# Two cross attentions: scores of two chunks together with their low part on halves of the array, and other places for the second loop's token and key work

## The reference, cut to what matters

```python
# inside the second block (a2): 32 wide heads, x [8,56,128], ee = ctx_512 [8,1500,64]
xn = _ln(x, lnx_g, lnx_b)
yn = _ln(y, lny_g, lny_b)
q = jnp.einsum('bsc,hcd->bhsd', xn, wq)
k = jnp.einsum('btc,hcd->bhtd', yn, wk)
v = jnp.einsum('btc,hcd->bhtd', yn, wv)
a = jax.nn.softmax(jnp.einsum('bhsd,bhtd->bhst', q, k) * D ** (-0.5), axis=-1)
o = jnp.einsum('bhst,bhtd->bhsd', a, v)
...
# the fifth block: 8 wide heads
qh = (q @ Wq + bq).reshape(B, LQ, HEADS, D_K).transpose(0, 2, 1, 3)
kh = (k @ Wk + bk).reshape(B, LKV, HEADS, D_K).transpose(0, 2, 1, 3)
vh = (v @ Wv + bv).reshape(B, LKV, HEADS, D_K).transpose(0, 2, 1, 3)
attn = jax.nn.softmax(jnp.einsum('bhqd,bhkd->bhqk', qh, kh) * scale, axis=-1)
out = jnp.einsum('bhqk,bhkd->bhqd', attn, vh)
```

## Time and profile before

| what | value |
|---|---|
| device time, median of 3 runs | 628.56 us (625.13 to 633.34) |
| the profiled execution, its time | 629.66 us |
| its span from first to last instruction | 627.8 us |
| first loop, a batch in the middle | 24.52 us |
| second loop, a batch in the middle | 22.69 us |
| PE, DVE, ACT, POOL busy over the span | 566.9, 444.7, 372.0, 380.6 us |

### The profile page before, as it was taken

One profiled execution on the slowest core, in us unless ns is written; L12 is line 12 of the kernel. 1 busy time (PEld: TensorE's weight loads), 2 busy tenths in 40 slices (PEclk: granted clock), 3 DMA queues, 4 the chain that ended last, 5 costly groups with the idle time before them and its releaser, 6 DMA issues.

```text
span 627.8 us, 18969 instructions
## 1 busy us (share of the span) xinstructions
PE 566.9 (90%) x8256; PEld 416.1 (66%) x8256; DVE 444.7 (71%) x698; ACT 372.0 (59%) x623; POOL 380.6 (61%) x271
## 2 busy tenths in 40 slices
PE   9788898899999999999888979977889889889897
PEld 4566775566767767666777556664667767778765
DVE  3876728697887887786356774776888988986543
ACT  2335674657657667566462417474677777777552
POOL 1572451488989889864630231175999999977500
PEclk9789999999999999999999999997999999999998
DMA  5830015002101101010013000412422432330000
GB/s 169 238 133 2 3 40 180 2 1 42 34 7 41 26 15 40 3 40 3 2 60 123 2 0 3 99 39 64 103 67 45 96 78 52 78 77 4 2 1 15
DMA packets 33838, 31.81 MB, mean 51 GB/s; under 512 B 27124, under 2 KB 27380, under 8 KB 33756
## 3 DMA queue, kind: packets, MB, share of 16 engines
q1 hardware_dynamic: 33756, 30.60, 18.8%
HBM read 13.06 MB, written 0.23 MB: 21 GB/s over the span
## 4 chain that ended last, share of the span: by engine, by line
PE 62%; DVE 18%; ACT 8%; issue 7%; POOL 3%; DMA 1%; DVEq 0%; POOLq 0%; ACTq 0%
PE psum L1143 9%; DVE scratch L1306 6%; PE psum L1067 5%; PE psum L1119 5%; PE psum L1503 4%; PE psum L1112 4%; PE psum L1114 4%; PE psum L1526 4%; DVE scratch L1291 4%; PE psum L217 3%; POOL scratch L1291 2%; ACT scratch L1276 2%; POOL scratch L652 1%; PE psum L1073 1%; PE psum L248 1%
## 5 line engine op out<-in xcount | busy, mean ns | idle before, releaser
L1291 POOL TENSOR_TENSOR scratch<-scratch 125x896 bf16<-125x896 f32 x143 | 242.7, 1715 | 80.4 <-ACT scratch L1276 79.9
L1306 DVE TENSOR_REDUCE scratch<-psum 128x1 f32<-128x500 f32 x336 | 210.3, 672 | 23.1 <-PE psum L1067 9.6
L1276 ACT ACTIVATE scratch<-psum 125x896 f32<-125x896 f32 x192 | 173.6, 917 | 82.8 <-PE psum L1143 51.1
L1112 PE MATMUL psum<-tok_high,scratch 125*128 125x65 bf16 x1344 | 107.0, 194 | 3.3 <-issue 2.7
L1114 PE MATMUL psum<-tok,scratch 125*128 125x64 bf16 x1344 | 106.4, 194 | 0.0
L1112 PEld LDWEIGHTS psum<-tok_high,scratch 125*128 125x128 bf16 x1344 | 94.8, 98 | 13.9 <-ACT scratch L1276 6.0
L1114 PEld LDWEIGHTS psum<-tok,scratch 125*128 125x128 bf16 x1344 | 88.6, 98 | 17.1 <-issue 0.5
L1143 PE MATMUL psum<-scratch 65*128 65x448 bf16 (+1 forms) x384 | 87.3, 352 | 0.0
L1291 DVE TENSOR_TENSOR scratch<-scratch 125x896 bf16<-125x896 f32 x49 | 67.5, 1383 | 22.8 <-ACT scratch L1276 21.1
L1119 PE MATMUL psum<-tok_high,scratch 125*128 125x65 bf16 x1344 | 72.7, 194 | 4.8 <-POOL scratch L1291 3.1
L1503 PE MATMUL psum<-scratch 128*128 128x500 bf16 x168 | 64.2, 382 | 10.8 <-DVE scratch L1306 6.5
(11 more groups left out here) (340 smaller groups left out, 870.5 us busy)
## 6 DMA issues: line engine op xcount, KB each, us to landing
nrm<-scratch SPq DMA_DIRECT2D x64, 96.0 KB, 2.2
nrm<-w_third SPq DMA_DIRECT2D x32, 96.0 KB, 2.2
raw<-ctx_dram SPq DMA_DIRECT2D x4, 672.0 KB
w_third<-fifth_dram SPq DMA_DIRECT2D x3, 595.0 KB, 6.0
w_third<-third_dram SPq DMA_DIRECT2D x2, 844.0 KB, 8.9
w_third<-third_dram SPq DMA_DIRECT2D x2, 843.5 KB, 6.8
w_fourth<-fourth_dram SPq DMA_DIRECT2D x3, 542.5 KB, 5.8
scratch<-scratch SPq DMA_DIRECT2D x8, 192.0 KB, 2.6
```

The costliest lines, as they stand in the source:

```text
L1112: nc.tensor.matmul(psum[:, sums, 65 * r:65 * r + 65], rows, t1[:, c, :], start=(c == 0 and r == 0), stop=False, skip_group_check=True)
L1276: nc.scalar.activation(CR["p"][0:CP, n % RING, :].rearrange("p (f n) -> p f n", f=2), psum[0:CP, S:S + 2, 0:HALF], ACT.Exp).then_inc(self. ...
L1291: ops.tensor_tensor(CR["pl"][0:CP, n % RING, :], CR["p"][0:CP, n % RING, :], p_high(n % RING), ALU.subtract).then_inc(done, 1)
L1306: nc.vector.tensor_reduce(mxp[:, r, t:t + 1], bank(B, TB), X_AXIS, ALU.max).then_inc(self.aux_freed, 1)
```

## The change

First loop. `scores_pe` does two chunks at each even step and nothing at the odd one: four matmuls over 128 rows, then four over 64 rows. The tiles `yb` and `qb` now hold the operands twice over: rows 0 to 63 for the first 448 columns, rows 64 to 127 for the second, so that these matmuls use one half of the array each. The row of ones and the shift move from row 64 to rows 0 and 64. For this channel 0 of the tokens has to go from the low product: `fold_keys_pool` subtracts the key weights' column 0 from all, once, on POOL. SP copies `yb` by two DMAs, 63 rows each. The shift is made and copied in halves of 448. Before it, ACT waits for DVE's low part of the queries.

Both loops. The rounding of the tokens to bfloat16 goes from POOL to ACT (`high_tokens`). POOL keeps the scaling (chunk 1) and the low parts: in the first loop both in chunk 11, in the second both in chunk 5. ACT does its part in chunks 4 and 5 of the first loop, 2 and 4 of the second.

Second loop. DVE does the roundings of chunks 5 and 6 instead of 1 and 2 (1 and 2 still in batch 0). The maxima are spread otherwise, the three key units of batch 0 stand in chunks 0 and 1, and SP turns the tokens of batch 2 before the groupings of batch 1.

```diff
+        def fold_keys_pool(pool):
+
+
+            keys = par("a2_wk").rearrange("p (h d) -> p h d", d=65)
+            nc.gpsimd.tensor_copy(keys[:, :, 64:65], keys[:, :, 0:1]).then_inc(key_scaled, 1)
+            pool.wait_ge(key_scaled, 2)
+            nc.gpsimd.tensor_tensor(keys[:, :, 0:64], keys[:, :, 0:64], keys[:, :, 64:65].to_broadcast([128, HEADS, CD]),
+                                    ALU.subtract).then_inc(key_scaled, 1)
+            pool.wait_ge(key_scaled, 3)
+
...
+                for k in range(2):
+                    nc.gpsimd.memset(CR["yb", i][64 * k:64 * k + 1, :].bitcast(F32), ONES).then_inc(y_ones, 1)
+                    pool.wait_ge(y_ones, 2 * i + k + 1)
...
+                    for r in range(3 * k, 3 * k + 4):
+                        lo, hi = max(128 * r, HALF * k), min(128 * r + 128, HALF * k + HALF)
+                        mm = nc.tensor.matmul(psum[:, B, lo - HALF * k:hi - HALF * k],
+                                              nmx[:, r:r + 1].to_broadcast([128, 128]),
+                                              ident16[:, lo - 128 * r:hi - 128 * r], start=True, stop=True)
...
+                if n % 2:
+                    return
+                b, i = n // CHUNKS, n // CHUNKS % 2
...
+                for m in (n, n + 1):
+                    if m >= 2:
+                        pe.wait_ge(self.probs, m - 1)
                     for f in range(2):
-                        mm = nc.tensor.matmul(bank(S + f, HALF), lhs[0:rows, 128 * c:128 * c + 128],
-                                              rhs[0:rows, HALF * f:HALF * f + HALF],
-                                              start=(rows == 128), stop=(rows != 128), skip_group_check=True)
-                return mm
+                        nc.tensor.matmul(bank(2 + 2 * (m % 2) + f, HALF), CR["ya", i][:, chunk(m)],
+                                         CR["qa", i][:, HALF * f:HALF * f + HALF], start=True, stop=False,
+                                         skip_group_check=True)
+                if n % CHUNKS == 0:
+                    self.wait_freed(pe, self.index("A", 1, b))
+                    pe.wait_ge(self.yb_in, 32 * (b + 1))
+                    pe.wait_ge(self.front_low, 2)
+                for m in (n, n + 1):
+                    for f in range(2):
+                        rows = slice(64 * f, 64 * f + 64)
+                        mm = nc.tensor.matmul(bank(2 + 2 * (m % 2) + f, HALF), CR["yb", i][rows, chunk(m)],
+                                              CR["qb", i][rows, HALF * f:HALF * f + HALF], start=False, stop=True,
+                                              skip_group_check=True)
+                        if f:
+                            mm.then_inc(self.scores, 1)
...
-                    if n >= 2:
-                        pe.wait_ge(self.probs, n - 1)
...
-                    mm = self.scores_pe(pe, n)
-                    mm.then_inc(self.scores, 1)
+                    self.scores_pe(pe, n)
...
-            def shift_row(self, i):
-                return CR["qb", i], 64
+            def shift_row(self, i, k):
+                return CR["qb", i], 64 * k
...
-                    tile, row = self.shift_row(i)
+                    if b and self is cross1:
+                        self.wait_freed(act, self.index("Q", 1, b))
+                    lo, hi = HALF * k, HALF * k + HALF
+                    tile, row = self.shift_row(i, k)
...
+                if c in (4, 5) and b < BATCH - 2:
+                    self.high_tokens(act, b + 2, c - 4)
...
-                    nc.vector.tensor_tensor(CR["qb", i][0:64, cols], bank(B, HALF, 64), CR["qa", i][0:64, cols],
-                                            ALU.subtract).then_inc(self.aux_freed, 1)
+                    nc.vector.tensor_tensor(CR["qb", i][64 * k:64 * k + 64, cols], bank(B, HALF, 64),
+                                            CR["qa", i][0:64, cols], ALU.subtract).then_inc(self.aux_freed, 1)
...
+            def scale_tokens(self, pool, b, k):
+                at = slice(CHUNKS * b + 6 * k, CHUNKS * b + 6 * k + 6)
+                nc.gpsimd.tensor_tensor(nrm[:, at, :], nrm[:, at, :], bc(crstd[:, at], CD), ALU.mult
+                                        ).then_inc(tok_scaled, 1)
+
...
-                    nc.gpsimd.tensor_tensor(src, src, bc(crstd[:, at], CD), ALU.mult).then_inc(tok_scaled, 1)
+                    self.scale_tokens(pool, b, k)
                     pool.wait_ge(tok_scaled, 2 * b + k + 1)
...
+                self.low_tokens(pool, b, k)
+
+            def high_tokens(self, act, b, k):
+
+                at = slice(CHUNKS * b + 6 * k, CHUNKS * b + 6 * k + 6)
+                act.wait_ge(self.pv_done, CHUNKS * (b - 2))
+                if self is cross1:
+                    act.wait_ge(tok_scaled, 2 * b + k + 1)
+                nc.scalar.activation(tok[b % TOKENS][:, 6 * k:6 * k + 6, 64:128], self.src[:, at, :], ACT.Copy
+                                     ).then_inc(self.tok_high, 1)
+
+            def low_tokens(self, pool, b, k):
+                i, lot = b % TOKENS, slice(6 * k, 6 * k + 6)
                 pool.wait_ge(self.tok_high, 2 * b + k + 1)
-                nc.gpsimd.tensor_tensor(tok[i][:, lot, 0:64], src, tok[i][:, lot, 64:128],
-                                        ALU.subtract).then_inc(self.tok_set, 1)
+                nc.gpsimd.tensor_tensor(tok[i][:, lot, 0:64], self.src[:, CHUNKS * b + 6 * k:CHUNKS * b + 6 * k + 6, :],
+                                        tok[i][:, lot, 64:128], ALU.subtract).then_inc(self.tok_set, 1)
...
+                    if b < BATCH - 2:
+                        self.tokens_pool(pool, b, c)
+
+            def tokens_pool(self, pool, b, c):
+
+                if c == 1:
+                    if b == 2:
+                        pool.wait_ge(cx_rstd, 2)
+                    for k in range(2):
+                        self.scale_tokens(pool, b + 2, k)
+                if c == CHUNKS - 1:
+                    for k in range(2):
+                        self.low_tokens(pool, b + 2, k)
...
-                sp.dma_start(CR["yb", b % 2][0:64, :], CR["ya", b % 2][64:128, :]).then_inc(self.yb_in, 16)
+                if b:
+                    sp.wait_ge(self.yb_in, 32 * b)
+                for k in range(2):
+                    sp.dma_start(CR["yb", b % 2][64 * k + 1:64 * k + 64, :], CR["ya", b % 2][65:128, :]
+                                 ).then_inc(self.yb_in, 16)
...
+            units_last, second_high = (), (2, 3)
...
-                return [("K", k) for k in range(3)] + FRONT[2:], (1, 2), (1, 2)
+                return [("K", k) for k in range(3)] + FRONT[2:], (5, 6)
...
-                    for c, n in enumerate((2, 1, 1, 2, 3, 3, 3, 2, 2, 1, 1) if b else (0, 0, 0, 0, 3, 3, 3, 3, 3, 3, 3)):
+                    for c, n in enumerate((2, 1, 2, 3, 3, 1, 1, 3, 2, 2, 1) if b else (0, 0, 1, 3, 3, 3, 3, 2, 2, 2, 2)):
                         at[c] += [[left.pop(0)] for _ in range(n)]
...
-                    if b == 0 and c < 3:
-                        lots += [[], [], [("K", c)]]
+                    if b == 0 and c < 2:
+                        lots += [[("K", 0)], [("K", 1)]] if c == 0 else [[("K", 2)]]
...
+            def low_on_pool(self, n):
+                if n < CHUNKS:
+                    return n not in (1, 2)
+                return super().low_on_pool(n)
+
+            def tokens_pool(self, pool, b, c):
+
+                if b == 0 and c in (1, 2):
+                    self.split_tokens(pool, 2, c - 1)
+                if b and c == 5:
+                    for k in range(2):
+                        self.low_tokens(pool, b + 2, k)
...
+                if b and c in (2, 4) and b < BATCH - 2:
+                    self.high_tokens(act, b + 2, c // 2 - 1)
...
+                if b == 1:
+                    cross2.turn_tokens(sp, 2)
                 cross2.group_keys(sp, b)
-                if 0 < b < BATCH - 1:
+                if 1 < b < BATCH - 1:
                     cross2.turn_tokens(sp, b + 1)
...
+            fold_keys_pool(pool)
```

50 lines of the change are left out of this document (17 added, 33 removed).

## The result

The changed kernel takes 653.77 us (median of 4 executions, 648.39 to 655.11) against 629.33 us before (625.13 to 633.34): ratio 1.0365, 95% interval 1.0313 to 1.0416. It is slower by 24 us. The forecast was 628 in a range of 613 to 640, so the size and the sign were wrong, and the time lies above the range.

The account below looks back on a forecast made before the run. PE was taken to bound the first loop, with no engine full in the second. Terms -1.3 - 4.5 + 6.2 - 1.0 = -0.6 took the profiled 629.66 to 629.1 us, 628 beside the median; range 613 to 640.

Parts of the forecast that it names:

- Second loop, batches 1 to 5: Second loop: the later token work makes each batch 23.9 instead of 22.7 us, +1.25, five times +6.2 us.
- The gate: Second loop, batches 1 to 5: the late token turn holds the first key unit until 16.1 us after the batch's first scores.
- one of two: Second loop: one of POOL's two low parts, beside a DVE rounding, takes 1.64 instead of 0.92 us.
- rival B: Second loop: waiting about 1.7 us before the first key unit lowers PE's clock, 2.5 a batch, +12.5, 641 us; chance 0.06.
- The first loop's second copy into yb: First loop, SP: a second small DMA per batch costs nothing, its data being needed a batch later.
- Second loop, batch 0: Turning batch 2's tokens before the groupings removes the 3.9 us wait and the half clock: -4.5 us, bounds -6.5 and -3.
- First loop: Paired scores on row halves save 1.0 us a batch, new waits take most back: -1.3 us in all.
- the two waits: First loop, PE: new wait of 0.70 us for an exponential, and 0.99 instead of 0.22 before the shift unit, +0.77.
- Batches 6 and 7: Second loop: moving DVE's roundings to chunks 5 and 6 removes half a wait in each batch, -1.0 us for both.
- The work in front: Ahead of the first loop: POOL's two added operations on the keys cost nothing; uncovered, 2.5 us.
- C: First loop: the array's halves don't overlap, 48 pairs x 0.22 = +10.6 instead of -1.3, 639 us; chance 0.06.
- A: Both loops: all gains arrive, first-loop waits covered and second loop not gated, -16, 613 us; chance 0.14.

Follow-up runs that it names:

- e4: The changed kernel with 26 unused matmuls filling PE's wait ahead of the first key unit in second-loop batches 1 to 5: 644.86 us, ratio 1.0243.
- e3: The changed kernel with the second loop's token work in chunk 3 instead of 5 (ACT's part in chunks 2 and 3): 639.60 us, ratio 1.0153.
- e13: The kernel before with only the second loop as changed, run again: 643.97 us, ratio 1.0158.
- e6: First loop as changed but without pairs, each chunk's scores alone with row halves; second loop as before: 632.51 us, ratio 1.0025.
- e7: First loop as changed with its output unit moved from chunk 5 into the wait ahead of the shift; second loop as before: 630.07 us, ratio 1.0001.
- e16: Second loop as changed; first loop's scores in pairs but with full rows and one copy into yb: 649.79 us, ratio 1.0378.
- e15: Second loop as changed; first loop as before except the copy into yb by two DMAs, eight more in the program: 651.58 us, ratio 1.0368.
- e8: First loop as before; second loop as changed, but DVE rounds chunks 3 and 4 and token work is in chunk 2: 627.74 us, ratio 0.9956.

## Why the prediction was wrong, point by point

**Second loop, batches 1 to 5** (+6.2 forecast, +23.7 measured). This is the term that failed. The gate was seen rightly: the late turn holds K 0, which puts the sign on this side. Two steps behind it were wrong: the size of the gate (12.6 us for the waits, 6.2 forecast), and a clock taken as held behind it (11.1 us, nothing in the sum); both sizes are from the profile with the wait filled (e4).

The gate: roundings until S + 10.0 (S + 9.8 measured), two low parts 2.5 us (3.48), landing 3.7 (3.7), K 0 at S + 16.1, by its own terms S + 16.35 (S + 17.5). The step is "one of two" low parts beside DVE's rounding; DVE has two roundings there, one for each. Another 0.5 us passes between the landing and K 0, and the landing of batch 1 took 4.7. With the clock held, a batch in the middle lasts 24.9 where 23.9 was said; the 7.8 us behind K 0 measured 7.5. The Trainium skill, SBUF — State Buffer, Summary: rules for kernel authors, says that beside a DVE operation with two SBUF inputs the second to issue is blocked until the first ends; as an estimate by it both low parts would wait for DVE's 1.09 and 1.21, which with the 1.79 of e3 is 4.1 us in all. The trace has 3.48, between the rule and what was taken.

The larger part of the miss is the clock. The prediction priced it as rival B, +2.5 a batch (2.4 measured) and gave it 0.06, because PE waits 1.20 us at 493.88 with the clock at 1.00. That row was no bound for this wait: B was priced for 1.7 us of waiting, and with the gate a microsecond later the wait is 3.1, much nearer to the 3.90 us that did take the clock down in the same trace. An error of a microsecond in the gate should have been carried into the rival's condition, not only into its own term.

**The first loop's second copy into yb** was priced at nothing: "its data are needed a batch later". That is so, and it costs the first loop nothing. But the eight DMAs make a landing in the second loop later, and with them the second half kept its clock in none of four executions (mean 0.963 at most): 9.6 us more than without them by the medians. The way from the DMAs to the clock stays open.

**Second loop, batch 0** (-4.5 forecast, -1.2 measured). The wait at 426 is gone as said. In e13 the same code had 25.7 (-4.5), with the turn alone 26.39 (-3.8). In the profile of the changed kernel the difference is the clock, 0.50 in two stretches, and a wait of 2.05 at the second key unit, since DVE's subtraction waits for the groupings:

```profile
424.63 0.60 PE L1576 MATMUL psum<-scratch 128*128 128x500 bf16 x1 [0.95 <-DVE scratch L1336]
...
436.97 0.75 DVE L1644 SCALAR_TENSOR_TENSOR w_third<-psum,w_third,scratch 128x512 bf16<-128x512 f32 x1 [2.64 <-DMA nrm<-scratch]
...
437.77 0.39 PE L1566 MATMUL psum<-scratch,w_third 128*128 128x512 bf16 x1 [2.05 <-DVE w_third L1644]
```

"The groupings are now 1.0 us later" was too little: the subtraction is at S + 20.9, not S + 18.5, and 1.8 us of that are the landing above (4.0 against 2.2).

**First loop** (-1.3 forecast, +3.2 measured). The pair was right (1.36 forecast, 1.35 measured), the halves overlap, and the two switches take 0.20 together (e6: 0.77 less 0.38 and 0.19). So were the two waits: 0.70 for the exponential (0.51), and 1.61 us from the last maximum to the shift, of which PE waits 0.81 by its row and 0.97 counted from the starts of the matmuls, as the forecast of 0.99 was. What failed is the sum: -1.0 + 0.70 + 0.77 - 0.2 is +0.3 a batch by the prediction's own terms, and the text took -0.1 from a placing of the pairs that it didn't show. Measured is +0.42. Missing was the wait of 0.20 for DVE. Batch 0 was counted like the others, but ACT has two more copies there: +1.4. The last batch was right (-0.6 forecast, -0.5).

**Batches 6 and 7** gave -0.8 and +0.4 instead of -1.0. The work in front cost nothing that can be seen: the first loop starts 0.5 us later, but over all profiles it starts between 113.3 and 119.5, and at 113.8 in one with this work (e7).

**The chances.** B had 0.06 and came, by its mechanism and in part: it was to explain 641, and the clock alone is half of the loss. C, that the halves take turns, is ruled out by the 1.35 us; A by the waits.

## What to carry to other kernels

When a chain is found to gate a unit, add up its slack from the worst neighbour of each link, and then ask what the wait does to the clock: here 3.1 us of waiting cost 2.2 us a batch by itself and 2.4 more behind it. Work that leaves an engine should land where the next work of that engine is someone else's: the same low parts cost a wait for SP's turn in chunk 5, a wait for POOL in chunk 3, and neither in chunk 2 with DVE rounding 3 and 4 and few maxima behind it. Doing two chunks at once shortens the work and takes away the slack between them; put other work, here the outputs, into the hole that it makes. Two changes that are measured together should be measured apart as well: here the good part of one (the early turn, the tokens' move) needed the other undone.

## What the runs showed of the hardware

The granted clock behind one and the same wait is not the same in each execution: behind 1.91 us it fell in one batch and stayed behind 1.92 in the next, behind 2.95 it fell and behind 2.91 it stayed in one execution (e16), behind 1.21 it fell in the run with the early turn and behind 1.20 it stayed in before, and the mean clock of one program ran from 0.955 to 0.983 (e13), but with eight DMAs more, elsewhere, from 0.955 to 0.963 (e15). Filling the 3.1 us with 26 matmuls whose results nobody uses kept it at 1.00 and narrowed the times of one program from 12 us to 5. Operations of POOL and DVE with two operands lengthen each other, and which side pays differs: two low parts on POOL took 3.48 us instead of 1.79 while DVE's roundings beside them took 1.09 and 1.21; in e8 DVE's rounding took 2.31 beside one of POOL's, which kept its 1.65; in e3 both paid, POOL's 2.52 and DVE's 1.60 and 1.97.

A 96 KB copy by SP landed 3.2 to 4.0 us after its issue where a 16 KB packet of the instruction queue fell on it, and 2.2 where none did. Not each such packet shows: of the second loop's transposing DMAs with a packet of the instruction queues beside them some landed after 3.7 us and some after 4.6 or more.
